# Two more split tiles a chunk, layer 0's first routing steps at tile 12, layer 1's selection and ranks later

## What is computed

```python
xn = _layernorm(x)                                   # layer 0
x = x + L0_attn(xn, W_qkv, W_out)                    # linear attention, 16 heads of 8, rope
      + L0_ffn(xn, router_w, e_bias, Wg, Wu, Wd, SWg, SWu, SWd)
#   scores = sigmoid(xn @ router_w.T); sfc = scores + e_bias
#   group score = sum of the two best of 8 experts; 4 of 8 groups stay; top 8 of 64 experts
#   coef[t, e] = 2.5 * score / sum of the chosen scores, zero for the others
#   h = silu(xn @ Wg[e]) * (xn @ Wu[e]) * coef[:, e];  out = sum over e of h @ Wd[e], plus a shared expert
xn = _layernorm(x)                                   # layer 1
x = x + L1_attn(xn, ...)                             # top 8 keys of 256, and a window of 4 neighbours
      + L1_ffn(xn, gate_w, w1, w2, w3)               # 8 experts of 256, the 2 best of a token
```

## Time and profile before

| | |
|---|---|
| median of three runs | 1735.33 us (1731.75 to 1736.39) |
| the profiled execution's own time | 1732.96 us |
| its span, first to last instruction | 1731.1 us |
| TensorE busy | 1663.4 us, 96% |
| VectorE busy | 1384.4 us, 80% |
| ScalarE busy | 906.6 us, 52% |
| mean granted TensorE clock | 0.991 |

### The profile page before, as it was taken

The page is one execution under the profiler, slowest core; times in us unless marked ns, Lnnn a source line. Parts: engine busy times, 40 slices in busy tenths (PEclk is TensorE's granted clock), DMA queues, the critical chain, the costliest instruction groups (busy, mean ns, idle before and its releaser), DMA issues.

```text
span 1731.1 us, 25092 instructions
## 1 busy us (share of the span) xinstructions
PE 1663.4 (96%) x7212; PEld 1224.1 (71%) x7212; DVE 1384.4 (80%) x3680; ACT 906.6 (52%) x1582; POOL 659.7 (38%) x637
## 2 busy tenths in 40 slices
PE   6999999999999999999999999999999998888877
PEld 4677777777777777777777777777777766656654
DVE  5778888888888888888888888888988884544438
ACT  5546564646464646464646464646464544433322
POOL 4421242424242525252525252524251434555650
PEclk9999999999999999999999999999999999999999
DMA  8858564646464646464646464646464455657538
GB/s 223 190 123 234 121 176 118 178 112 185 111 186 108 187 107 187 106 188 107 185 102 172 105 171 108 166 112 164 108 164 109 115 164 178 212 191 238 180 129 312
DMA packets 172438, 273.94 MB, mean 158 GB/s; under 512 B 14408, under 2 KB 57416, under 8 KB 172048
## 3 DMA queue, kind: packets, MB, share of 16 engines
q1 hardware_dynamic: 163728, 254.63, 55.1%
q0 software_dynamic: 8576, 17.70, 3.2%
HBM read 202.15 MB, written 65.93 MB: 155 GB/s over the span
## 4 chain that ended last, share of the span: by engine, by line
PE 87%; DVE 4%; ACT 3%; another core or an unknown queue 2%; issue 2%; DMA 1%; SPq 0%; POOL 0%; ACTq 0%; DVEq 0%; POOLq 0%
PE ps_y L801 16%; PE ps_gate L742 8%; PE ps_gate L740 8%; PE ps_gate L741 8%; PE ps_up L740 7%; PE ps_up L742 7%; PE ps_up L741 7%; PE ps_y L827 3%; PE ps_side L755 3%; PE ps_y L793 2%; PE ps_y L791 2%; PE ps_y L790 2%; PE ps_side L850 1%; PE ps_side L944 1%
## 5 line engine op out<-in xcount | busy, mean ns | idle before, releaser
L1025 DVE TENSOR_TENSOR silu_h<-ps_up,silu_h 128x512 f32<-128x512 f32 x618 | 420.9, 683 | 265.4 <-ACT silu_h L1456 156.1
L1456 ACT ACTIVATE silu_h<-ps_gate 128x512 f32<-128x512 f32 x618 | 366.9, 597 | 432.2 <-PE ps_gate L742 355.4
L801 PE MATMUL ps_y<-silu_h,w_dn 128*128 128x512 f32 x672 | 342.8, 591 | 0.2 <-DVE silu_h L1013 0.2
L1013 DVE TENSOR_TENSOR silu_h<-coef_b,silu_h 128x1024 f32<-128x1024 f32 x256 | 328.6, 1284 | 4.8 <-DMA coef_b<-coef_kept 4.1
L740 PE MATMUL ps_gate<-xnT,w_gu 128*128 128x512 f32 x528 | 309.6, 586 | 0.0
L740 PE MATMUL ps_up<-xnT,w_gu 128*128 128x512 f32 x528 | 207.7, 393 | 3.2 <-DVE silu_h L1025 3.2
L741 PE MATMUL ps_gate<-xnT,w_gu 128*128 128x512 f32 x528 | 208.3, 394 | 0.0
L742 PE MATMUL ps_gate<-xnT,w_gu 128*128 128x512 f32 x528 | 208.2, 394 | 0.0
L742 PE MATMUL ps_up<-xnT,w_gu 128*128 128x512 f32 x528 | 207.7, 393 | 0.0
L741 PE MATMUL ps_up<-xnT,w_gu 128*128 128x512 f32 x528 | 207.0, 392 | 0.0
L1747 POOL DMA_INDIRECT slots_x<-rows,slot_of x120 | 162.4, 1353 | 90.6 <-PE ps_gate L742 68.9
(11 more groups left out here) (289 smaller groups left out, 3013.7 us busy)
## 6 DMA issues: line engine op xcount, KB each, us to landing
coef_b<-coef_kept SPq DMA_DIRECT2D x254, 512.0 KB
slots_x<-empty SPq DMA_DIRECT2D x15, 2080.0 KB, 12.8
w_block<-w_kept SPq DMA_DIRECT2D x45, 512.0 KB
xs<-slots_x SPq DMA_DIRECT2D x37, 260.0 KB
y_back<-y_kept SPq DMA_DIRECT2D x15, 512.0 KB, 6.9
w_down<-in_ffn_w SPq DMA_DIRECT2D x45, 128.0 KB
w_raw<-in_ffn_w SPq DMA_DIRECT2D x33, 128.0 KB, 7.7
xres<-in_x SPq DMA_DIRECT2D x16, 256.0 KB, 3.1
```

Source lines behind the costliest of these rows:

```text
L801: eng.matmul(ps_y[:, :], down_of(j), silu_h[:, h_at(g)], start=j == 0, stop=last).then_inc(pe_down)
L1013: eng.tensor_tensor(silu_h[:, s:s + 2], coef_b[:, q % COEF_RING, k:k + 2], silu_h[:, s:s + 2], ALU.mult).then_inc(dve_h)
L1025: eng.tensor_tensor(silu_h[:, s], ps_up[g % 2][:, :], silu_h[:, s], ALU.mult).then_inc(dve_h1)
L1456: eng.activation(silu_h[:, s], ps_gate[g % 2][:, :], ACT.Silu).then_inc(act_silu)
```

## The change

Three things change together.

- Tiles 21 and 25 become split as singles, so 14 of 33 tiles are split. Single tiles now take the two halves of `h_hi` in turn (`half_of`), and the copy into a half waits for the down product that last used that half (`half_user_before`).
- In `ROUTE0`, `choice`, `pair4`, `pair2` and `pair1` move from tiles 18, 18, 19, 20 to tile 12. Chunk 0 keeps them at tile 18 (`ROUTE0_SECOND`).
- In `ROUTE1`, `select` moves from tile 30 to tile 3 of the next chunk and `prefix` from tile 31 to tile 4 of it; `rank` moves from tile 6 to 7 and `key` from tile 7 to 8; `first2` stays at 8 and `slot` at 9.

Beside these some buffers are placed elsewhere, and the first loads of the down weights of the single tiles go to `msg` and not to `yT`, so that the first `y_out` no longer waits.

```diff
-SPLIT_GROUPS = [(0, 1), (4, 5), (8, 9), (15,), (19,), (23,), (27,), (30, 31)]
+SPLIT_GROUPS = [(0, 1), (4, 5), (8, 9), (15,), (19,), (21,), (23,), (25,), (27,), (30, 31)]
...
 ROUTE0 = [(0, "stats0"), (2, "norm0"), (4, "xT0"), (5, "x_lo0"), (8, "vr0"), (8, "vr1"), (9, "score"),
-          (18, "choice"), (18, "pair4"), (19, "pair2"), (20, "pair1"), (21, "gtop"), (22, "gstrike"), (23, "groups"), (24, "top8"),
+          (12, "choice"), (12, "pair4"), (12, "pair2"), (12, "pair1"), (21, "gtop"), (22, "gstrike"), (23, "groups"), (24, "top8"),
...
-ROUTE1 = [(5, "stats1"), (7, "norm1"), (8, "xT1"), (9, "x_lo1"), (10, "vl0"), (10, "vl1"), (11, "top1"), (12, "gate_exp"), (23, "softmax"), (30, "select"),
-          (31, "prefix"), (39, "rank"), (40, "key"), (41, "first2"), (42, "slot"), (43, "send0"), (45, "send1"), (47, "send2"), (48, "send3"),
+ROUTE1 = [(5, "stats1"), (7, "norm1"), (8, "xT1"), (9, "x_lo1"), (10, "vl0"), (10, "vl1"), (11, "top1"), (12, "gate_exp"), (23, "softmax"), (36, "select"),
+          (37, "prefix"), (40, "rank"), (41, "key"), (41, "first2"), (42, "slot"), (43, "send0"), (45, "send1"), (47, "send2"), (48, "send3"),
...
+        def half_of(j):
+
+            return SPLIT_SINGLES.index(j) % 2 if j in SPLIT_SINGLES else j % 2
+
+        def half_user_before(g):
+
+            c, j = tile_of(g)
+            k = [j in group for group in SPLIT_GROUPS].index(True)
+            both = j in SPLIT_PAIRS or SPLIT_GROUPS[k - 1][0] in SPLIT_PAIRS
+            return groups_before(g) - (1 if both else 2)
...
             def round_ready(g):
-                n = groups_before(g)
+                n = half_user_before(g)
                 eng.wait_ge(dve_h, scaled_before(g) + 1)
-                if n > 0:
-                    eng.wait_ge(pe_down, last_of_group(n - 1) + 1)
+                if n >= 0:
+                    eng.wait_ge(pe_down, last_of_group(n) + 1)
...
             def y_out(c):
                 if c > 0:
                     eng.wait_ge(*done("yT", c - 1))
-                if c == 0:
-                    eng.wait_ge(dve_wds, 2)
```

More of the change, by code:

```diff
@@ L43 @@
 RUNS = [[range(0, 2)], [range(2, 4)], [range(4, 6)], [range(6, 8)], [range(8, 10)],
-        [range(10, 15), range(16, 19), range(20, 23), range(24, 27), range(28, 30), range(32, 33)], [range(15, 28, 4), range(30, 32)]]
+        [range(10, 15), range(16, 19), range(20, 28, 2), range(28, 30), range(32, 33)], [range(15, 16), range(19, 28, 2), range(30, 32)]]
 RING = 4
@@ L82 @@
 ROUTE0 = [(0, "stats0"), (2, "norm0"), (4, "xT0"), (5, "x_lo0"), (8, "vr0"), (8, "vr1"), (9, "score"),
-          (18, "choice"), (18, "pair4"), (19, "pair2"), (20, "pair1"), (21, "gtop"), (22, "gstrike"), (23, "groups"), (24, "top8"),
+          (12, "choice"), (12, "pair4"), (12, "pair2"), (12, "pair1"), (21, "gtop"), (22, "gstrike"), (23, "groups"), (24, "top8"),
           (25, "strike"), (26, "weigh"), (28, "coefT")]
-ROUTE0_SECOND = [(at + 6 if at < 10 else at + 1 if at < 14 else at, what) for at, what in ROUTE0]
-ROUTE1 = [(5, "stats1"), (7, "norm1"), (8, "xT1"), (9, "x_lo1"), (10, "vl0"), (10, "vl1"), (11, "top1"), (12, "gate_exp"), (23, "softmax"), (30, "select"),
-          (31, "prefix"), (39, "rank"), (40, "key"), (41, "first2"), (42, "slot"), (43, "send0"), (45, "send1"), (47, "send2"), (48, "send3"),
+ROUTE0_SECOND = [(at + 6 if at < 14 else at, what) for at, what in ROUTE0]
+ROUTE1 = [(5, "stats1"), (7, "norm1"), (8, "xT1"), (9, "x_lo1"), (10, "vl0"), (10, "vl1"), (11, "top1"), (12, "gate_exp"), (23, "softmax"), (36, "select"),
+          (37, "prefix"), (40, "rank"), (41, "key"), (41, "first2"), (42, "slot"), (43, "send0"), (45, "send1"), (47, "send2"), (48, "send3"),
           (49, "send4"), (51, "send5"), (53, "send6"), (54, "send7")]
@@ L237, in build_program @@
         w_kvr = sb("w_kvr", [2 * P + EXPERTS0])
+        at_plain = ExitStack()
+        counted = sb("counted", [EXPERTS1, 16], within=at_plain)
+        upto = sb("upto", [EXPERTS1, EXPERTS1], within=at_plain)
+        past = sb("past", [BLOCKS1, EXPERTS1], within=at_plain)
+        at_plain.close()
         x_plain = sb("x_plain", [CHUNK])
@@ L284, in build_program @@
         slot_of = sb("slot_of", [2, ROWS, TOP1], INT32)
-        sb("gap", [24])
-        counted = sb("counted", [EXPERTS1, 16])
+        sb("gap", [128])
         tiles_e = sb("tiles_e", [EXPERTS1])
-        upto = sb("upto", [EXPERTS1, EXPERTS1])
         ends = sb("ends", [EXPERTS1])
-        past = sb("past", [BLOCKS1, EXPERTS1])
         expert_of = sb("expert_of", [BLOCKS1])
@@ L784, in last_products @@
                 if split_h(g):
-                    n, k = groups_before(g), j % 2
+                    n, k = groups_before(g), half_of(j)
                     eng.wait_ge(dve_wds, 2)
@@ L1412, in single_rest @@
                 eng.wait_ge(act_hhi, groups_before(g) + 1)
-                eng.tensor_tensor(h_lo[:, s], silu_h[:, s], f32(h_hi[:, 1]), ALU.subtract).then_inc(dve_hlo)
+                eng.tensor_tensor(h_lo[:, s], silu_h[:, s], f32(h_hi[:, half_of(tile_of(g)[1])]), ALU.subtract).then_inc(dve_hlo)
             eng.memset(minus_half[:, :], -0.5)
@@ L1477, in single_round @@
                 round_ready(g)
-                eng.copy(h_hi[:, 1], silu_h[:, h_at(g)]).then_inc(act_hhi)
+                eng.copy(h_hi[:, half_of(tile_of(g)[1])], silu_h[:, h_at(g)]).then_inc(act_hhi)
             def y_out(c):
```

2 lines of the change are left out of this document (1 added, 1 removed).

## The result

The changed kernel takes 1755.07 us (median of 4 runs, 1753.66 to 1756.72) against 1734.96 us for the kernel before, run beside it: ratio 1.0119, 95% interval 1.0104 to 1.0134. That is 20.1 us slower, where I had forecast 8 us slower; the direction was right and the time lies outside the range. The profiled execution has a span of 1754.5 us at a mean granted clock of 0.987.

What follows compares the result with a forecast made beforehand. The prediction took TensorE's own queue to bound the fifteen steady chunks. Its terms, +14.6 us of waits less 6.0 us saved, gave +8.6 us and a forecast of 1743 us, range 1734 to 1750 us.

Steps and rivals of the forecast that it cites:

- Two more split tiles, 6.0 us off TensorE's queue: Two tiles in each of chunks 1 to 15: 0.20 us saved a tile, 6.0 us off TensorE's queue.
- `rank` and `key` one tile later, +14.6 us: Tile 8, chunks 2 to 14: `xT1` waits for `left` to release its bank, 1.10 us a chunk, 14.6 us.
- DVE cannot begin the stretch earlier: DVE ahead of `left`: everything from `times_up` of tile 5 on is tied to ACT's silu, after 2.59 us of waiting.
- a bound of `times_coef`: Tile 8: `times_coef` stretched like chunk 2's `h_lo` (1.69 us against 1.23) gives a 1.56 us wait, 20.6 us in all.
- rival 3: `times_coef` of tiles 6 and 7 slows under POOL, 0.46 us more each: +14.6 us, 1748 to 1750 us; chance 0.08.
- What the split tiles cost elsewhere: nothing: Two new `h_lo` add 1.2 us to DVE a chunk; with the cover 0.96 us stay spare at tile 28.
- the tightest consumer: Up product of tile 30, which needs `times_up` of tile 28: 1.13 us spare before the change.
- The cover: Choice steps moved to tile 12 put DVE 1.43 us further ahead from tile 21, paying the new `h_lo` (1.2 us).
- `select` and `prefix`, the choice at tile 12: nothing: The moved DVE steps fit into holes of 3.52 us (tile 13) and 2.59 us (tile 5); cost nothing.
- The rest, 0 +- 0.5 us: Chunk 0 rounds two more down weights and drops one ACT wait, both once: 0 +- 0.5 us.
- my +8.6 us: Whole kernel: the forecast's sum, +14.6 us for the wait at `xT1` less 6.0 us for the split tiles.
- Rivals 1 and 2: Tile 8: no bank wait, 1727 to 1729 us (0.12); or half the wait, 1733 to 1736 us (0.07).

Runs made afterwards that it cites:

- minimum early: The changed kernel with POOL's minimum `k_min` of layer 0 at tile 4 instead of 6; ratio 1.0103 to the kernel before, +17.4 us.
- ranks alone: The kernel before with only `rank` and `key` one tile later (40 and 41); ratio 1.0103 to the kernel before, +17.4 us.
- ranks back: The changed kernel with `rank` and `key` one tile earlier again (39 and 40); ratio 1.0019 to the kernel before, +3.2 us.

## Why the prediction was right in direction and wrong in size

1. *Two more split tiles, 6.0 us off TensorE's queue.* Right: 5.9 us (0.20 and 0.19 a chunk), and the two intervals in which their down products now run, behind the up products of 25 and 29, are 2.04 and 2.06 us in every chunk.
2. *`rank` and `key` one tile later, +14.6 us.* The mechanism was right in every link, and undoing it takes 17 us away. The price was right for the edit alone (14.7 us in its trace), too low in the changed kernel: 17.7 us. The step that failed is the stretch's starting point, "DVE cannot begin the stretch earlier": it can begin later. It starts with the pair `h_lo`, which starts together with POOL's L1707 (L1696 before) and takes 1.23 or 1.69 us by which of them is held. I had the 1.69 us and used it for a bound of `times_coef`, and in rival 3, at the wrong instruction: `times_coef` of 6 and 7 takes 1.22 or 1.23 us in every chunk. Where `h_lo` was the one held, POOL is through by then; in the seven other chunks L1707 still has 0.73 us to run beside it, and neither is longer for it. The rule that I cited from the Trainium skill (GPSIMD Engine Reference, section 1, Specifications), that the two engines contend when VectorE reads two SBUF inputs, is borne out by these traces two instructions further up and again at tile 30. It is not borne out by this last overlap, so it does not say by itself which overlap costs.
3. *What the split tiles cost elsewhere: nothing.* This is the step that failed outright, 6.4 us. I took the up product of tile 30 as "the tightest consumer" and `times_up` of tile 28 as its supplier, and added up DVE's lateness as if each instruction kept its duration. That sum was good: in chunk 7 `times_coef` of 26 and 27 starts 1.11 us ahead of the up product of tile 30 and started 1.27 us ahead before, 0.16 us less, where the prediction had 1.13 - 0.96 = 0.17 us. But the 0.60 us put between `msg` and `times_coef` let POOL start first, and 0.88 us more of duration broke the down product of tile 26. The two experiments that keep the instruction and part the engines, one from each side, both take the wait away in chunks 1 to 14. The 0.5 us of chunk 15 stay, so they are not shown to be POOL's.
4. *The cover.* That the choice's relief pays for the new `h_lo` was right, and more important than I had it: without it I priced the new tiles at +7.1 us of waits, less 6.0 saved; they cost +21.1 us. I had counted one consumer; there are two, the second `h_lo` itself and `times_coef` behind it. The relief is counted in the wrong place too: what counts is DVE's position when it reaches tiles 27 and 28, and that differs by 1.44 us (1.23 + 0.21).
5. *`select` and `prefix`, the choice at tile 12: nothing.* Right from chunk 1 on (+1.7 us in all for both, and tile 20 of chunk 0 alone is 1.8).
6. *The rest, 0 +- 0.5 us.* Off by 1.2 us in chunk 0, and by the 0.7 us of tile 14 of chunk 3 and tile 10 of chunk 15. The text ahead of the prediction says that chunk 0 keeps the steps at tile 18; that holds for `choice` and `pair4`. `pair2` and `pair1` were at 19 and 20 there and now stand at 18, all ahead of `times_up` of tile 19. I had the new rule before me and did not apply it step by step.

Together: 17.7 + 6.4 - 5.9 + 1.2 + 0.7 = 20.1 us, and the medians differ by 20.1 us. That the two agree to the digit is luck: the two profiled executions differ by 23.4 us, with the 3.2 us behind the last chunk. Of the 11.5 us above my +8.6 us, 6.4 are tile 30 and 3.1 the longer wait at tile 8. Rivals 1 and 2 asked for a shorter wait than 1.10 us, and no chunk of any kernel with the later ranks and a `key` had one but chunk 2 of minimum early (0.91 us, where the wait is set against an `h_lo` that was long before). Open are what stretches chunk 0's tiles 7 to 9 by up to 2.5 us in some executions, and what stretches tile 10 of chunk 15 by 0.2 us in every kernel with the later ranks.

## What to carry to other kernels

An instruction put into a busy queue costs more than its own length when it shifts the next one past the start of another engine's work on the same memory: list, for each instruction that it delays, what GpSimd starts within that instruction's time, and who is first. Moves that bring nothing alone can be what a third change needs, so price a change as a whole and take it apart by single undoing. And for a queue that is 97% busy, ask where it stands against its consumer at the end of the stretch, not how busy it is.

## What the runs showed of the hardware

An instruction of VectorE with two inputs in SBUF and one of GpSimd can hold each other up. At tile 30 the starts lie 0.3 us apart and the one that starts first keeps its time: `times_coef` takes 1.21 us first and 2.09 us second, the addition 1.29 us first and 2.05 us second. The pair `h_lo` takes 1.23 us beside a minimum (L1707, L1696 before) of 2.58 us, or 1.69 us beside one of 1.51. In the changed kernel's chunk 7 and in that of ranks alone the two starts are within 0.01 us of each other, and the order on record does not tell who wins: in chunks 4 and 12 to 14 of the changed kernel `h_lo` starts 0.002 us ahead and is held, in chunk 7 of ranks alone it starts 0.002 us ahead and is not. The same kernel had eight held pairs in one execution and three in the other.

Who starts first is not the whole rule either. The held `h_lo` loses 0.46 us, not the minimum's whole 1.51. In chunk 3 of the changed kernel the pair of tiles 8 and 9 starts 0.81 us ahead of POOL's L1713 and is held all the same (1.70 and 2.24 us). And `times_coef` of tiles 6 and 7 starts beside the last 0.73 us of L1707 and takes 1.22 or 1.23 us, while L1707 takes 2.58 us as it does where only 0.13 us of it overlap, before. `times_up`, which reads PSUM and SBUF, took 0.67 to 0.69 us beside either.

The two levels of time differ by 47 us on the same kernel, about as much as the part behind the last chunk does, where layer 1's weights are streamed: 314.2 us there for the kernel before, 266.1 to 267.2 us for the seven kernels profiled at the shorter level. What makes the levels is not shown; it is not the chip alone, since the kernel before took 1685.9 and 1731.9 us under one and the same chip number. Windows over the same 100 us, first of the kernel before at the longer level, then of ranks back at the shorter:

```profile
1500.00:1600.00 100.00, 85.02 (x364) 58.10 (x363) 44.88 (x110) 34.15 (x61) 57.40 (x61) 0.97 0.65 213
```

```profile
1500.00:1600.00 100.00, 100.00 (x453) 70.94 (x452) 57.49 (x130) 43.74 (x77) 72.87 (x77) 1.00 0.79 257
```

The one moves 213 GB/s and leaves TensorE idle for 15 us, the other 257 GB/s with TensorE busy throughout.
